# Two graph layers on one core: normalized h turned by VectorE and DMA instead of TensorE

## What is computed

```python
def _L0_gnn_ref(x, adj, Wq_w, Wq_b, Wk_w, Wk_b, Wv_w, Wv_b):
    query = jnp.einsum('bnd,od->bno', x, Wq_w) + Wq_b
    keyt = jnp.einsum('bnd,od->bno', x, Wk_w) + Wk_b
    value = jnp.einsum('bnd,od->bno', x, Wv_w) + Wv_b
    weight = adj * jnp.exp(jnp.einsum('bqd,bkd->bqk', query, keyt))
    weight = weight / jnp.sum(weight, axis=2, keepdims=True)
    return jnp.einsum('bqk,bkd->bqd', weight, value)

def _L1_gnn_ref(x, adj, W):
    deg = jnp.sum(adj, axis=-1, keepdims=True)
    agg = jnp.einsum('bij,bjf->bif', adj, x) / jnp.maximum(deg, 1e-6)
    return jax.nn.relu(jnp.einsum('bnf,of->bno', jnp.concatenate([x, agg], axis=2), W))

# x: 64 graphs x 256 nodes x 512, adj: 64 x 256 x 256, all float32
h = jnp.maximum(_layernorm(x), 0.0);  x = x + _L0_gnn_ref(h, adj, ...)
h = jnp.maximum(_layernorm(x), 0.0);  x = x + _L1_gnn_ref(h, adj, L1_gnn_W)
```

## Time and profile before

| | |
|---|---|
| median of 3 runs | 2045.35 us (2045.01 to 2046.1) |
| profiled execution, its own time | 2044.76 us |
| its span | 2043.0 us |
| TensorE matmul busy | 2023.5 us, 99% |
| VectorE, ScalarE, GpSimd busy | 1419.1, 774.2, 1015.3 us |
| DMA | 155.30 MB, mean 76 GB/s |
| the chain that ended last | 97% TensorE |

### The profile page before, as it was taken

The page is one execution under the profiler, slowest core; times in us unless marked ns, Lnnn a source line. Parts: engine busy times, 40 slices in busy tenths (PEclk is TensorE's granted clock), DMA queues, the critical chain, the costliest instruction groups (busy, mean ns, idle before and its releaser), DMA issues.

```text
span 2043.0 us, 28487 instructions
## 1 busy us (share of the span) xinstructions
PE 2023.5 (99%) x9852; PEld 1704.6 (83%) x9852; DVE 1419.1 (69%) x2329; ACT 774.2 (38%) x1289; POOL 1015.3 (50%) x958
## 2 busy tenths in 40 slices
PE   8899999999999999999999999999999999999999
PEld 5688888888888888888888888888888888888887
DVE  6877666776667776667767677766677676777654
ACT  3433444333443334443334433344433344333432
POOL 3555554555544555545555445555455554455520
PEclk9899999999999999999999999999999999999999
DMA  5122122212222221222122222212221222222101
GB/s 191 62 70 76 63 81 92 82 51 72 77 87 82 69 75 63 81 92 82 51 72 77 87 82 70 74 63 81 92 82 51 72 77 87 82 69 75 64 30 52
DMA packets 114753, 155.30 MB, mean 76 GB/s; under 512 B 10800, under 2 KB 75312, under 8 KB 114736
## 3 DMA queue, kind: packets, MB, share of 16 engines
q1 hardware_dynamic: 114736, 155.08, 22.6%
HBM read 121.38 MB, written 33.68 MB: 76 GB/s over the span
## 4 chain that ended last, share of the span: by engine, by line
PE 97%; DVE 2%; issue 0%; DMA 0%; SPq 0%; ACT 0%; ACTq 0%
PE bank L337 31%; PE bank L339 31%; PE bank L338 31%; PE bank L345 3%; DVE h L732 0%; PE bank L467 0%; PE bank L468 0%; DMA x_in<-x 0%; DVE w_l L175 0%; DVE w L747 0%; DVE hT_l L691 0%; DVE v_l L686 0%; DVE stats L696 0%; DVE n_l L686 0%; DVE hT_l L686 0%
## 5 line engine op out<-in xcount | busy, mean ns | idle before, releaser
L292 POOL TENSOR_TENSOR xT<-xT,shared 128x512 f32<-128x512 f32 x248 | 455.5, 1873 | 162.2 <-DMA shared<-norms 162.2
L325 POOL TENSOR_TENSOR at_l<-adjT,at_h 128x1024 fp32r<-128x1024 f32 x32 | 81.4, 2543 | 323.4 <-ACT at_h L677 323.4
L581 ACT ACTIVATE y<-bank 128x512 f32<-128x512 f32 x128 | 76.7, 599 | 370.7 <-PE bank L339 370.7
L732 DVE CUSTOM_DVE_ANT_0 h<-h,u_b,bqk 128x512 f32<-128x512 f32 x128 | 215.1, 1733 | 0.0
L175 POOL TENSOR_TENSOR w_l<-w,w_h 128x512 fp32r<-128x512 f32 x62 | 80.3, 1295 | 257.2 <-ACT w_h L599 257.2
L337 PE MATMUL bank<-hT_h,n_h 128*128 128x512 f32 x512 | 200.2, 391 | 0.8 <-DVE hT_l L686 0.5
L269 POOL TENSOR_TENSOR rs<-var_eps,minus_half 128x2 f32<-128x2 f32 x128 | 89.5, 699 | 222.5 <-DVE var_eps L708 222.5
L339 PE MATMUL bank<-hT_h,n_l 128*128 128x512 f32 x512 | 199.8, 390 | 0.0
L338 PE MATMUL bank<-hT_l,n_h 128*128 128x512 f32 x512 | 199.8, 390 | 0.0
L337 PE MATMUL bank<-wv_h,hT_h 128*128 128x512 f32 x512 | 199.2, 389 | 0.0
L338 PE MATMUL bank<-wv_l,hT_h 128*128 128x512 f32 x512 | 199.2, 389 | 0.0
(11 more groups left out here) (125 smaller groups left out, 4883.6 us busy)
## 6 DMA issues: line engine op xcount, KB each, us to landing
x_in<-x SPq DMA_DIRECT2D x32, 1024.0 KB, 5.4
xT<-x_t SPq DMA_DIRECT2D x62, 512.0 KB, 6.8
out<-x SPq DMA_DIRECT2D x124, 256.0 KB, 2.0
adjT<-adj_t SPq DMA_DIRECT2D x32, 512.0 KB, 3.6
shared<-adj SPq DMA_DIRECT2D x32, 512.0 KB, 4.6
shared<-norms SPq DMA_DIRECT2D x31, 512.0 KB, 3.6
x<-wq SPq DMA_DIRECT2D x4, 256.0 KB, 3.9
xb<-wk SPq DMA_DIRECT2D x4, 256.0 KB, 5.0
```

The source lines that it names most:

```text
L292: pool.tensor_tensor(tile, tile, norms[:, k * T:(k + 1) * T, :], (ALU.mult, ALU.add)[k]).then_inc((xT_scaled, xT_shifted)[k], 1)
L325: pool.tensor_tensor(at_l[:, :, :], adjT[:, :, :], at_h[:, :, :].bitcast(F32), ALU.subtract).then_inc(at_split, 1)
L581: nc.scalar.activation(y[:, :], bank[L1_BANK][:, :], ACT.Copy).then_inc(ha_copied, 1)
L732: nc.vector.tensor_tensor_reduce(h[:, t, :], h[:, t, :], u_b[:, :], 1.0, bqk[:, 0:1], ALU.mult, ALU.add, key_bias[:, t:t + 1]).then_inc(ke ...
```

## The change

The transposed copy of x is no longer read, and the normalization is no longer applied to it. h itself is turned for both layers:

- VectorE transposes every 32x32 block of a tile of h in place of its block (new `turn`), one instruction for a tile, into `blocks`, which holds the two tiles of one graph.
- SP stores `blocks` to DRAM with 4 DMAs of 128 KB (`store_blocks`), waits for them, and loads it back with one DMA of 512 KB into `turned` (`load_turned`), by which each block comes to the partitions where it belongs. `blocks` has one buffer: the second graph of a pair is turned only when the first is stored. All four such round trips of a step (two layers, two graphs) go through SP's queue.
- ScalarE copies a tile of `turned` to hT_h or gT_h; GpSimd makes the low part (`low_tile`), 8 tiles in a step. The low parts of hT and gT leave VectorE, and `xT_step` leaves GpSimd.
- TensorE's turns go from steps 1 to 31. Those of the first pair for layer 0 and of the last pair for layer 1 stay. `v(0)` moves ahead of `scores(0)` and `v(1..3)` ahead of z; kp goes to banks 7, 4, 5, 6.
- ScalarE's relu of the next pair goes ahead of the high parts of z(0) and z(1), in pairs of tiles. Key biases of tiles 1 to 3 move behind the results of layer 1. adj is loaded into w's place.

```diff
+            def store_blocks(k, g, blocks_done, count, stored):
+                sp.wait_ge(blocks_done, count)
+                for jj in range(P // Q):
+                    sp.dma_start(turned_d[k, g, jj].rearrange("a i n -> i a n"),
+                                 blocks[:, jj].rearrange("p c t b -> p (c t b)")).then_inc(stored[g], 16)
+            def load_turned(k, g, stored, count, moved):
+                sp.wait_ge(stored[g], 64 * count)
+                sp.dma_start(turned[:, g].rearrange("p i c t b -> p (i c t b)"),
+                             turned_d[k, g].rearrange("j a i n -> (j a) (i n)")).then_inc(moved[g], 16)
...
             def step(i, layer0=True, layer1=True, more=True):      # SP
-                    sp.wait_ge(xT_shifted, DT * (i if layer0 else i - 1))
-                    sp.dma_start(adj_in, adj_d[j]).then_inc(adj_loaded, 16)
+                if layer0 and layer1:
+                    store_blocks(1, 0, g_turned, T * j + NT, g_stored)
+                    load_turned(1, 0, g_stored, j + 1, g_moved)
                 if layer1 and more:
                     load_x(i + 1)
-                    load_xT(i + 1)
-                if more:    (store and broadcast of norms)
+                if layer0 and layer1:
+                    store_blocks(1, 1, g_turned, T * (j + 1), g_stored)
+                    load_turned(1, 1, g_stored, j + 1, g_moved)
+                if more:
+                    store_blocks(0, 0, ...); load_turned(0, 0, ...)
+                    store_blocks(0, 1, ...); load_turned(0, 1, ...)
+                if layer0:
+                    sp.wait_ge(sum_split, i + 1)
+                    sp.dma_start(adj_in, adj_d[i]).then_inc(adj_loaded, 16)
...
+            def low_tile(dst, high, t, high_done, count, done):     # GpSimd
+                pool.wait_ge(high_done, count)
+                pool.tensor_tensor(by_blocks(dst, t), turned_tile(t), by_blocks(high, t).bitcast(F32),
+                                   ALU.subtract).then_inc(done, 1)
...
                 if layer1:                                          # GpSimd's step
+                    low_gT(j, 0)
+                    low_gT(j, 1)
+                    split_w(pool, i, 0)
+                    low_gT(j, 2)
+                    low_gT(j, 3)
                 if layer1 and more:
                     scale_and_shift(0, i + 1)
-                    xT_step(i + 1, 0)
+                if layer1:
+                    split_w(pool, i, 1)
                 (sum_l)
                 if more:
-                    xT_step(i + 1, 1)
+                    for t in range(T):
+                        low_hT(i + 1, t)
...
+                    for dt in range(DT):                            # TensorE's step
+                        kp(dt)
+                    v(0)
                     scores(0)
-                        turn_g(j, 2)
-                        turn_g(j, 3)
                     scores(1)
+                    for t in range(1, T):
+                        v(t)
...
+                    high_v(0)                                       # ScalarE's step
+                        high_gT(0); high_gT(1)
                     exp(0)
                     exp(1)
                     high_w(0)
+                        high_gT(2); high_gT(3)
                     high_w(1)
+                    high_v(1..3)
+                    next_h(0); next_h(1)
                     high_z(0)
+                    next_h(2); next_h(3)
                     high_z(1)
                     high_z(2)
...
+            def turn(t, done):                                      # VectorE
+                nc.vector.transpose(blocks[:, :, :, t % NT, :].rearrange("p j c b -> p c j b"),
+                                    h[:, t, :].rearrange("p (c j b) -> p c j b", c=DT, b=Q)).then_inc(done, 1)
+            def turn_h(i, g):
+                dve.wait_ge(h_done[0], T * i + NT * (g + 1))
+                if g:
+                    dve.wait_ge(h_stored[0], 64 * i)
...
                     low_kp(1)
+                        turn_g(j, 0)
                     low_kp(2)
                     low_kp(3)
+                        turn_g(j, 1)
+                    low_v(0)
                     weigh(0)
+                        layer0_stats(i + 1, 0)
                     weigh(1)
+                        layer0_stats(i + 1, 1)
+                    low_v(1); low_v(2); low_v(3)
                     low_z(0)
+                    turn_h(i + 1, 0)
                     low_z(1)
                     low_z(2)
+                    turn_h(i + 1, 1)
                     low_z(3)
+                    key_bias_of(i + 1, 0)
```

More of the change, by code:

```diff
@@ L281, in add_bv, with low_gT, low_hT @@
                     pool.tensor_tensor(xb[:, t, :], x_in[:, t, :], bv_b[:, :], ALU.add).then_inc(xb_done, 1)
[L283 to L293, removed]
+            def low_tile(dst, high, t, high_done, count, done):
+                pool.wait_ge(high_done, count)
+                pool.tensor_tensor(by_blocks(dst, t), turned_tile(t), by_blocks(high, t).bitcast(F32),
+                                   ALU.subtract).then_inc(done, 1)
+            def low_gT(j, t):
+                low_tile(gT_l, gT_h, t, gT_high, T * j + t + 1, gT_split)
+            def low_hT(i, t):
+                low_tile(hT_l, hT_h, t, hT_high, T * (i - 1) + t + 1, hT_split)
             pool.wait_ge(consts, 2)
@@ L423, in z @@
                 def z(t):
[L424 to L427, removed]
+                    if layer0:
+                        pe.wait_ge(gT_split, T * j + t + 1)
+                    elif t == 0:
+                        pe.wait_ge(last_split, DT)
+                    if t == 0 and first:
+                        pe.wait_ge(weight_split, PIECES)
                     if t >= 2:
@@ L434, in v @@
                 def v(t):
-                    if t == 0 and not layer1:
-                        pe.wait_ge(weight_split, 1)
+                    if t == 0:
+                        pe.wait_ge(*((x1_done, T * j + 1) if layer1 else (weight_split, 1)))
                     if t >= 2:
@@ L599, in high_w, with next_h @@
                     nc.scalar.activation(w_h[:, g], w[:, g], ACT.Copy).then_inc(w_high, 1)
+                def next_h(t):
+                    if t == 0 and layer1:
+                        act.wait_ge(g_turned, T * (j + 1))
+                    relu_norm(0, x_in, i + 1, t)
                 if layer0:
+                    high_kp(0)
                     if layer1:
@@ L605, in step @@
                         relu_norm(1, x1, j, 1)
-                    high_kp(0)
                     high_kp(1)
@@ L842, in step @@
                     low_kp(0)
-                    low_kp(1)
                     if layer1:
@@ L847, in step @@
                         layer0_stats(1, 0)
+                    low_kp(1)
+                    if layer1:
+                        dve.wait_ge(h_stored[1], 64 * i)
+                        dve.wait_ge(hT_split, T * i)
+                        turn_g(j, 0)
                     low_kp(2)
-                    if not layer1:
-                        layer0_stats(1, 1)
                     low_kp(3)
                     if layer1:
-                        low_gT(j, 0)
-                        low_gT(j, 1)
+                        turn_g(j, 1)
                     else:
+                        layer0_stats(1, 1)
                         low_weight(2)
-                        key_biases(0, 0, ahead=False)
-                        key_biases(0, 1)
+                        for t in range(T):
+                            key_bias_of(0, t, ahead=False)
+                    low_v(0)
                     weigh(0)
-                    if layer1:
-                        low_gT(j, 2)
-                        low_gT(j, 3)
+                    if layer1 and more:
+                        layer0_stats(i + 1, 0)
                     weigh(1)
@@ L894, in step @@
                         layer1_result(t)
-                        low_hT(i + 1, t)
                         if t == 1:
                             sum_inverses()
+                        if t > 0:
+                            key_bias_of(i + 1, t)
                 if layer0:
-                    if not layer1:
-                        for t in range(T - 1):
-                            low_hT(1, t)
                     if not (layer1 and more):
                         sum_inverses()
-                    if not layer1:
-                        low_hT(1, T - 1)
                     layer0_result(0)
```

276 lines of the change are left out of this document (142 added, 134 removed).

## The result

The changed kernel takes **2445.9 us** (median of 4 runs, 2442.19 to 2452.43) against 2045.7 before: a ratio of 1.196, interval 1.193 to 1.199. It is slower by 400 us. The forecast was 1994, range 1988 to 2040: wrong in sign and in size.

What follows compares the result with a forecast made beforehand. TensorE, busy 99% with a gapless list of matmuls, was taken as the bound. 2044.76 - 54.3 (turns) + 3.0 (head) + 0.1 (tail) = 1993.6; the median is 0.6 above: 1994 us, range 1988 to 2040.

Steps and rivals of the forecast that it cites:

- What leaves TensorE: The 16 turns of each of 31 steps go from TensorE, 1.75 us a step, 54.3 us in all.
- A group of four stores ... 3.5 us: On SP's queue, four stores issue 0.5 us apart and the last lands 2.0 later: 3.5 us.
- The prediction's own sign of being wrong: The prediction falls if TensorE waits in every step for kz_l (z(2) or az(0)), or for exp in v(2).
- the round trips are slow: Rival: four stores and a load take 5.4 us each, z(2) waits 2.7, low_z(3) is late; 2102 us, chance 0.17.
- a bound of 27.5: The kernel turns slower once layer 1's second load lands past 27.5 us into the step.
- The tight place: Behind layer 1's second load, 7.25 us of work end low_z(0) at 31.5; z(2) wants it at 32.95: 1.5 to spare.
- Prices without a row: Prices taken: 0.7 us for VectorE's turn of a tile, 1.3 for GpSimd's low tile, 3.6 for a 512 KB load.
- The rival of turns twice as long: VectorE's turn takes 1.4 us a tile: 2033 us; with lesser delays 2003 to 2041, partial losses, chance 0.24.
- the 2025: Time estimated from the skill page's 311 ns for VectorE's transpose, four in a row, 1.24 us a tile.
- The head: At the start, kp of step 1 begins at 75.6, 1.0 later, partly at the lower clock: +3.0 us together.
- The chances: Turns and trips as priced 0.56, partial losses 0.24, no change 0.03, slower 0.17.

Runs made afterwards that it cites:

- experiment 9: experiment 5 with VectorE's low_z(3) ahead of the second turn, low_z(1) ahead of the first, and ScalarE's high_z(1) ahead of next_h(2): 1999.44 us.
- experiment 1: The changed kernel with each group's four stores cut by 32 node partitions, so the outermost dimension is 32 and not 4: 2047.15 us.
- experiment 5: experiment 1 with ScalarE's high part of z(0) ahead of the relu of the next pair's first two tiles: 2007.09 us.
- experiment 4: experiment 1 with x's load moved behind the second graph's store and load in SP's order: 2047.65 us.
- experiment 7: The changed kernel, its stores on four engines as they are, with only ScalarE's high part of z(0) moved ahead of the relu: 2452.01 us.

## Why the prediction was wrong, point by point

**What leaves TensorE: right.** 1.75 us a step was forecast, 62.42 - 60.68 = 1.74 is measured where nothing waits (experiment 9).

**"A group of four stores ... 3.5 us": the step that failed.** It was priced by out's landing of 2.0 us, a transfer of the same kind, to DRAM, of twice the bytes of one store. But bytes and direction were not what set the price. It took 7.9 us on four engines, 3.6 on sixteen. With it, 2446; with the same bytes on all engines, 2047 (experiment 1). The prediction's own sign of being wrong, a wait for kz_l in every step, is there: z(2) waits in all 31.

**The rival "the round trips are slow" had the mechanism, not the size.** It gave 5.4 for a group, 2102, and a bound of 27.5 for the second high tile. The group took 7.9 and 11.3, the tile came at 34.0. The rival's argument, z(2) behind the second load and low_z(3) behind layer 0's store, is what the waits show (211 and 10 us). It left out two terms: exp and the copy of ha wait as well (29.5 and 70.6 us), and the clock. TensorE's busy time is 2086.2 us after and 1973.7 in experiment 9, for the same 9356 matmuls: 112.5 us more, 3.6 a step. Some 94 of them, by an estimate from the starts, are matmuls at the lower level: about 520 start 0.42 apart in place of 0.23, and 32 in experiment 9. Nearly all the rest comes of the records, since the last one ahead of a wait counts with its full 0.39 us and there are a hundred waits. 60.7 + 10.4 + 3.6 = 74.7, against steps of 74.3 to 77.4, 75.2 in the mean.

**"The tight place": mis-sized by 2 us.** Even with stores on 16 engines, low_z(0) came 0.6 too late instead of 1.5 early. In experiment 1 the second group lands 23.0 us into the step and not 20.5, and the high tile begins at 26.3 and not at 24.2. x's megabyte landed 7.3 us after its issue there, not 5.4. The sum had moved 2 MB at 379 GB/s, a rate of loads; with the stores among them the same 2 MB went at a mean of 251 (the second window of experiment 1). That the rate is lower for stores in general was not tried. From the high tile to the end of low_z(0) it took 7.2 us (1046.20 to 1053.43), as the 7.25 of the forecast: only the landings were off. Experiments 5 and 9 show that this place and its neighbour, z(3) behind the low part of z(1), were nearly all that was left.

**Prices without a row: right, nearly.** Turn 688 ns, low tile 1269 for gT, on which the tight place rests, but 1408 for hT, which had room to spare; load 3.3 us. The rival of turns twice as long (1.4 us a tile) did not come, and so neither did the cause of the 2025 that the forecast worked out from the figure of 311 ns of the Trainium skill, "VectorE: DVE Perf Modes", section "The three transpose paths"; that page's figure is for bf16 and 128x128, and the measured price of a whole 128x512 float32 tile decides.

**The head: nearly right.** Kp of step 1 was to start at 75.6. It started at 84.90 after (17 us of waiting for hT_l, behind two slow groups) and at 77.13 in experiment 9, with some fourteen matmuls at the lower level where 8 to 12 were forecast. Head and step together: 1994 with 1.5 more for the start, some 1.0 for the clock and 3.1 for a few steps that were up to 1.2 longer than 60.68 is 1999.6; 1999.44 was measured.

**The chances.** A group of stores between 3.5 and 5.4 us was not an interval from the trace: its upper end was another load's landing, and no row had a transfer with a short outermost dimension. An unknown price needed a bound by the number of engines, visible in the diff, and 0.17 was too little for a chain of four such trips.

## What to carry over

Price a transfer by its access pattern before its bytes: read the outermost dimension of both sides, and where it is 4, count on a quarter of the bandwidth (93 of 379 GB/s here); in a window in which only that transfer runs, the DMA share shows it at once. In a chain with 1.5 us to spare, put what TensorE waits for next ahead of work for the next pair on each engine's queue; here such exchanges were worth 48 us once the stores ran on all engines, and the first of them nothing while they ran on four. A wait that is removed is worth only as much as the next one in line is later: experiments 4 and 7 moved a wait and gained nothing.

## What the runs showed that was not expected

- A kernel with short waits is less steady than one without: experiment 1, with 29 waits of up to 2.6 us, had runs from 2037 to 2057 us; experiment 9 had 1998.5 to 2000.2.
- Waits cost more than their length. In experiment 1, 28.5 us of waiting for kz_l came with 10.5 us more busy time of the same matmuls than in experiment 9 (1984.2 against 1973.7). By an estimate from the starts, some 6 us of it are matmuls at the lower level, and most of the rest is the overlap of records that a wait undoes.
- Twice as many engines gave nearly twice the rate (47 and 93 GB/s), and a group fell from 14.0 to 7.9 us. Nearly all sixteen did not give four times as much again: the share was 0.93, but the rate 206 GB/s in the window shown, and a group still took 3.6 us, where 512 KB at the loads' 379 GB/s are 1.4. What holds the stores below the rate of loads is open.
